# A graph attention layer on one core: nodes laid on the partitions by fours in place of twos

## The reference

```
h      = max(layernorm(x), 0)
Wh     = h @ W
e      = leaky_relu((Wh @ a1)[:, None] + (Wh @ a2)[None, :], 0.2)
scores = where(adj > 0, e, -9e15)
out    = x + elu(softmax(scores, axis=1) @ Wh)
```

## Time and profile before

| what | value |
|---|---|
| median of 3 runs | 654.71 us (654.53 to 655.17) |
| the profiled execution's own time | 654.69 us |
| its span in the profile | 652.8 us |
| PE, DVE, ACT busy | 95%, 94%, 96% |
| POOL busy | 13% |
| DMA queue of GpSimd (loads of `adj`) | 98.6% of 16 engines' span |
| read from HBM | 270.60 MB |

### The profile page before, as it was taken

How to read it: one execution, slowest core, us unless ns; L and a number is a source line. 1 busy time by engine, 2 the same in 40 slices (tenths; PEclk the granted TensorE clock), 3 DMA queues, 4 the chain that set the end, 5 groups by cost and what they waited for, 6 DMA issues and landing times.

```text
span 652.8 us, 23363 instructions
## 1 busy us (share of the span) xinstructions
PE 618.5 (95%) x10422; PEld 607.1 (93%) x10422; DVE 614.8 (94%) x651; ACT 623.9 (96%) x357; POOL 81.6 (13%) x149
## 2 busy tenths in 40 slices
PE   4878999999999999999999999999999999989997
PEld 4748999999999999999899999999999999989997
DVE  5899999999999999889999999999999999999997
ACT  5799999899999999999999999999999999999992
POOL 7200200110110110100010110101010110011000
PEclk9987999999999999999999999999999999999999
DMA  9999999999999999999999999999999999999994
GB/s 173 109 108 109 110 108 108 110 109 109 109 108 108 107 107 108 108 108 108 107 108 108 108 108 107 108 107 108 108 108 107 108 107 108 108 108 107 107 97 132
DMA packets 27678, 71.81 MB, mean 110 GB/s; under 512 B 3200, under 2 KB 11136, under 8 KB 27648
## 3 DMA queue, kind: packets, MB, share of 16 engines
q0 software_dynamic: 18576, 67.12, 98.6%
q1 hardware_dynamic: 8608, 4.19, 2.4%
q10 hardware_dynamic: 464, 0.07, 0.1%
HBM read 270.60 MB, written 2.10 MB: 418 GB/s over the span
## 4 chain that ended last, share of the span: by engine, by line
ACT 53%; DMA 17%; PE 12%; issue 9%; DVE 7%; ACTq 1%; POOL 1%; DVEq 0%
ACT work L520 37%; DMA store<-in_adj 16%; ACT work L528 14%; DVE store L721 4%; PE psum L1083 3%; PE psum L1081 3%; PE psum L1061 2%; PE psum L1050 1%; PE psum L1028 1%; ACT last_steps L533 1%; DVE store L739 1%; DVE work L745 1%; DMA x_sb<-in_x 1%; PE psum L1018 1%; ACT V L512 1%
## 5 line engine op out<-in xcount | busy, mean ns | idle before, releaser
L520 ACT ACTIVATE work<-trow,Wh 128x4096 int8<-128x4096 f32 x128 | 494.6, 3867 | 0.0
L1081 PE MATMUL psum<-V,work 128*128 128x130 f16 x4096 | 479.3, 220 | 1.2 <-DVE work L745 1.2
L1083 PE MATMUL psum<-V,work 128*128 128x130 f16 x4096 | 479.2, 220 | 0.0
L1081 PEld LDWEIGHTS psum<-V,work 128*128 128x128 fp8e4 x4096 | 401.9, 98 | 1.5 <-issue 1.5
L1083 PEld LDWEIGHTS psum<-V,work 128*128 128x128 fp8e4 x4096 | 401.8, 98 | 0.0
L721 DVE TENSOR_SCALAR store<-store 128x4096 uint8<-128x4096 int8 x127 | 290.2, 2286 | 4.4 <-DMA store<-in_adj 4.4
L739 DVE SCALAR_TENSOR_TENSOR store<-work,store 128x1024 int32<-128x1024 int32 x128 | 156.5, 1222 | 12.7 <-ACT work L520 10.0
L528 ACT COPY work<-psum 128x1024 int32<-128x1024 int32 x128 | 147.5, 1155 | 7.6 <-PE psum L1061 7.4
L1061 PE MATMUL psum<-identb,store 128*128 128x128 bf16 x2048 | 135.7, 220 | 16.3 <-DVE store L739 13.4
L1061 PEld LDWEIGHTS psum<-identb,store 128*128 128x128 bf16 x2048 | 119.6, 98 | 20.1 <-DVE store L739 10.7
L443 POOL DMA_DIRECT2D store<-in_adj x127 | 71.2, 561 | 510.9 <-DVE store L721 503.3
(11 more groups left out here) (90 smaller groups left out, 146.6 us busy)
## 6 DMA issues: line engine op xcount, KB each, us to landing
store<-in_adj POOLq DMA_DIRECT2D x127, 512.0 KB, 27.6
x_sb<-in_x SPq DMA_DIRECT2D x4, 512.0 KB, 6.2
out_y<-x_sb SPq DMA_DIRECT2D x1, 1792.0 KB, 8.0
store<-in_adj POOLq DMA_DIRECT2D x2, 256.0 KB, 35.3
out_y<-x_sb SPq DMA_DIRECT2D x1, 128.0 KB, 6.0
out_y<-x_sb SPq DMA_DIRECT2D x4, 32.0 KB, 1.6
store<-in_L_gnn_W ACTq DMA_DIRECT2D x4, 16.0 KB, 5.3
a_sb<-in_L_gnn_a ACTq DMA_DIRECT2D x1, 0.5 KB, 4.2
```

The lines of the kernel that those rows point to most:

```text
L520: nc.scalar.activation(sign[:, k % 2].bitcast(I8), trow[:, h * UW:(h + 1) * UW], ACT.Sign, bias=(Wh[:, B, 0:1] if isinstance(B, int) else ...
L1081: nc.tensor.matmul(sums_of[:, 0], up8[:, j // 2, j % 2], V[:, jb, 0:FP], start=begins and j == 0, stop=False, skip_group_check=True)
L1083: last = nc.tensor.matmul(sums_of[:, 1], down8[:, j // 2, j % 2], V[:, jb, VP:VP + FP], start=False, stop=stops and j == HB - 1, skip_grou ...
```

## The change

Four neighbouring nodes share a partition in place of two: node `g * 512 + p * 4 + b` lies on partition `p` in block `4g + b`. The set of rows in a body stays the same; which of them form a tile changes. The rows of `adj` in one tile were rows `2p + b` of 256, so those of neighbouring partitions lay 2 rows (64 KB) apart; now they are rows `4p + b` of 512, 4 rows (128 KB) apart. Each row's piece is still 16 KB in memory. The loads of `x` and the large stores of the result have pieces of 1 KB (four rows) in place of 512 bytes. The transposes of the codes take every second bfloat16 word, and `spread` writes to every fourth word of `trow`. The products, their operands and their order in the queues stay as they are. The general path's loops run over 16 groups of four in place of 32 pairs, so each engine's code for it has four bodies in place of two.

```diff
-        adj_v = adj.rearrange("(i k p b) j -> k b i p j", p=P, b=2, k=KE // 2)
-        out_i = out.rearrange("(i w p b) f -> i p w b f", p=P, b=2, w=2)
+        adj_v = adj.rearrange("(i p b) j -> b i p j", p=P, b=KE)
+        out_i = out.rearrange("(i p b) f -> i p b f", p=P, b=KE)
...
-                xs = x.rearrange("(g p b) f -> p g b f", p=P, b=2)
-                with nc.allow_non_contiguous_dma(reason="pairs of rows of x, 512 bytes each"):
+                xs = x.rearrange("(g p b) f -> p g b f", p=P, b=KE)
+                with nc.allow_non_contiguous_dma(reason="four rows of x, 1 KB each"):
                     for r in range(NR):
-                        sp.dma_start(x_sb[:, out_of(r), :].rearrange("p (g b) f -> p g b f", b=2),
-                                     xs[:, r * PR:(r + 1) * PR]).then_inc(s_x[r], 16)
+                        sp.dma_start(x_sb[:, out_of(r), :].rearrange("p (g b) f -> p g b f", b=KE),
+                                     xs[:, r * RR // KE:(r + 1) * RR // KE]).then_inc(s_x[r], 16)
-                out_p = out.rearrange("(g p b) f -> p g b f", p=P, b=2)
+                out_p = out.rearrange("(g p b) f -> p g b f", p=P, b=KE)
...
-                    sp.dma_start(out_p[:, i * KE // 2:j * KE // 2],
-                                 x_sb[:, i * KE:j * KE, :].rearrange("p (g b) f -> p g b f", b=2)).then_inc(s_out, 16)
+                    sp.dma_start(out_p[:, i:j],
+                                 x_sb[:, i * KE:j * KE, :].rearrange("p (g b) f -> p g b f", b=KE)).then_inc(s_out, 16)
...
-                    sp.dma_start(out_i[NI - 1, :, b // 2, b % 2], x_sb[:, (NI - 1) * KE + b]).then_inc(s_last, 16)
+                    sp.dma_start(out_i[NI - 1, :, b], x_sb[:, (NI - 1) * KE + b]).then_inc(s_last, 16)
...
-                    pool.dma_start(adj_ring[:, k % RT, :].bitcast(F8W), adj_v[b // 2, b % 2][i, :, h * UW:(h + 1) * UW])\
+                    pool.dma_start(adj_ring[:, k % RT, :].bitcast(F8W), adj_v[b][i, :, h * UW:(h + 1) * UW])\
                         .then_inc(s_adj[k % RT], 16)
...
-                    nc.scalar.activation(trow[:, r * TR * P:(r + 1) * TR * P].rearrange("p (g q b) -> p g b q", q=P, b=2),
-                                         t_ps[r].rearrange("p (g b q) -> p g b q", q=P, b=2), ACT.Copy)\
+                    nc.scalar.activation(trow[:, r * TR * P:(r + 1) * TR * P].rearrange("p (g q b) -> p g b q", q=P, b=KE),
+                                         t_ps[r].rearrange("p (g b q) -> p g b q", q=P, b=KE), ACT.Copy)\
...
                     for g in range(GU):
-                        last = nc.tensor.transpose(into[:, g * P:(g + 1) * P], mine[:, g * P:(g + 1) * P], identb[:, :])
+
+                        c = g // 2 * 2 * P + g % 2
+                        last = nc.tensor.transpose(into[:, g * P:(g + 1) * P], mine[:, c:c + 2 * P - 1:2], identb[:, :])
```

More of the change, by code:

```diff
@@ L44, in build_gat @@
     HB = JB // 2
-    NW = JB // 2
     UW = N // 2
@@ L280, in rows @@
             return what[bass.ds(w, 1), b].rearrange("o p j -> p (o j)")
-        adj_b = adj.rearrange("(w p b) j -> w b p j", p=P, b=2)
-        x_b = x.rearrange("(w p b) f -> w b p f", p=P, b=2)
-        out_b = out.rearrange("(w p b) f -> w b p f", p=P, b=2)
+        adj_b = adj.rearrange("(w p b) j -> w b p j", p=P, b=KE)
+        x_b = x.rearrange("(w p b) f -> w b p f", p=P, b=KE)
+        out_b = out.rearrange("(w p b) f -> w b p f", p=P, b=KE)
         def general_sync(sp):
@@ L289, in general_sync @@
                 sp.sem_inc(g_out, ONE)
-                with sp.Fori(0, NW) as w:
-                    for b in range(2):
-                        sp.wait_ge(g_read, ONE + w * 2 + b)
+                with sp.Fori(0, NI) as w:
+                    for b in range(KE):
+                        sp.wait_ge(g_read, ONE + w * KE + b)
                         sp.dma_start(A, rows(adj_b, w, b)).then_inc(g_adj, 16)
-                        sp.wait_ge(g_res, ONE + w * 2 + b)
+                        sp.wait_ge(g_res, ONE + w * KE + b)
                         sp.dma_start(xt, rows(x_b, w, b)).then_inc(g_x, 16)
@@ L299, in general_scalar @@
                 all_done(act)
-                with act.Fori(0, NW) as w:
-                    for b in range(2):
-                        i = w * 2 + b
+                with act.Fori(0, NI) as w:
+                    for b in range(KE):
+                        i = w * KE + b
                         act.wait_ge(g_dve, i * DSTEPS + 6)
@@ L323, in general_vector @@
                 nc.vector.tensor_copy(Wh1, Wh[:, :, 3:FW]).then_inc(g_Wh1, 1)
-                with dve.Fori(0, NW) as w:
-                    for b in range(2):
-                        i = w * 2 + b
+                with dve.Fori(0, NI) as w:
+                    for b in range(KE):
+                        i = w * KE + b
                         def after(k):
@@ L371, in general_tensor @@
                 pe.wait_ge(g_Wh1, 1)
-                with pe.Fori(0, NW) as w:
-                    for b in range(2):
-                        i = w * 2 + b
+                with pe.Fori(0, NI) as w:
+                    for b in range(KE):
+                        i = w * KE + b
                         pe.wait_ge(g_res, ONE + i)
@@ L384, in general_tensor @@
                                 jb = r * RR + j
-                                c = jb // 2 * 2 * P + jb % 2
+                                c = jb // KE * KE * P + jb % KE
                                 last = nc.tensor.transpose(half[r % 2][:, j * P:(j + 1) * P],
-                                                           score[:, c:c + 2 * P - 1:2], ident[:, :])
+                                                           score[:, c:c + KE * (P - 1) + 1:KE], ident[:, :])
                             last.then_inc(g_round, 1)
@@ L463, in _ @@
                     pool.dma_start(adj_ring[:, RT - 1, n * TW // 2:(n + 1) * TW // 2].bitcast(F8W),
-                                   adj_v[b // 2, b % 2][NI - 1, :, h * UW + n * TW // 2:h * UW + (n + 1) * TW // 2])\
+                                   adj_v[b][NI - 1, :, h * UW + n * TW // 2:h * UW + (n + 1) * TW // 2])\
                         .then_inc(loaded, 16)
```

## The result

The changed kernel takes 656.18 us (median of 12 runs, 654.97 to 656.88) against 654.71 (654.45 to 655.22). The ratio is 1.002 with a 95% interval of 1.0013 to 1.0028: slower by 1.5 us, where 0.3 us less was forecast. The profiled execution took 656.88 us with a span of 654.8.

The account below looks back on a forecast made before the run. The prediction took the stream of `adj` loads to bound the kernel, with engines close behind. Its sum: 654.71 - 0.3 (start) + 0 (loads) + 0 (transposes) + 0 (spreads, 0.6 under cover) = 654.4 us; range 653.4 to 656.4.

Parts of the forecast that it names:

- What bounds the kernel: Whole run: the DMA stream of `adj` sets the end at 4.88 us a tile, engines close behind at 4.62 us a unit.
- Loads of `adj` at 0: 128 tile loads: rows 128 KB apart in place of 64 KB cost 0, as the DMA engines' pace looks constant.
- transposes at 0: TensorE's 2048 code transposes: a 4-byte step costs 0; at most 41 ns each, 84 us in all.
- The rule of the Trainium skill: Loads of `adj`: large power-of-two row distances lose rate; its table costs nothing at 128 KB. Rival of slower loads: 667 us, 6%.
- Load of `x`, 0.3 us: Start of the kernel: 1 KB pieces land `x` and start the `adj` loads 0.3 us earlier; bounds 0 and 1.1 us.
- The spreads: ScalarE's eight table copies: writing every fourth word costs another 78 ns each, 0.6 us in all, hidden by the cover.
- the upper bound: Spreads priced by L581's scattered access, 0.92 ns a word: 0.94 us a spread, 7.5 us in all.
- The cover: Whole run: how much slower the engines could be for nothing, about 1.8 us, from TensorE's idle time between 560 and 630 us.
- the spreads' rival: ScalarE's spreads much slower: tables ready 7.5 us later, 5.7 us come out, 660.1 us; chance 4%.
- Its small case: Slower spreads with only the last four on the path: 3.8 - 1.8 = 2.0 us come out, 656.4 us.
- the stated range: Kernel time from 653.4 to 656.4 us, a little beyond the likeliest case's 653.6 to 655.6.
- The signs of being wrong: Landings over 4.89 us apart: row distance; VectorE not waiting late, TensorE at 99%: engines; L503 near 2 us: spreads.

Follow-up runs that it names:

- the rows alone: Kernel before with only the loads of `adj` changed, taken from rows 128 KB apart: 654.74 us, ratio 1.0002.
- the experiment: Changed kernel with copies of 1024 words at various steps added ahead of the first spread; float32 writes four words apart cost 0.94 us more, kernel time not given.
- all spreads twice: Kernel before with a plain copy of 1024 words ahead of each of its eight spreads and a wait between: 657.99 us, ratio 1.005.
- the spreads alone: Kernel before with only its eight spreads changed, writing to every fourth word of `trow`: 655.54 us, ratio 1.0019.

## Why the prediction was wrong, point by point

- **What bounds the kernel: right.** The loads of `adj` set the end before, and the engines were close behind. Taking the first loads forward gained time, and delays of the engines cost none until they passed 3.85 us.
- **Loads of `adj` at 0, transposes at 0: right**, each shown alone on the chip. The rule of the Trainium skill (DMA: Bandwidth & Descriptors, Latency and other measured facts) on row distances, cited in the prediction, costs nothing at 128 KB here: 654.74 us and 108 GB/s with the rows alone.
- **Load of `x`, 0.3 us: right for the landing**, 4.29 in place of 4.62 over seven traces each. In the time of the kernel it isn't told from noise: with the spreads undone the rest of the change gives 654.59 against 654.66. Its issue also became cheaper, 2.33 us for four in place of 3.86.
- **The spreads: this step failed.** "I take another 78 ns each, 0.6 us in all." They cost 937 ns each (2032 - 1095), 7.5 us in all, which was the upper bound to the tenth. The value was carried on from a step of two words as if the further step cost as much as the first; instead the price comes in beyond 8 bytes and is full at 16. A row for the dear side was there: L581, which takes words 272 bytes apart, 0.92 ns each, and the experiment gives 0.92. I used it as the bound and chose the other. The Trainium skill (SBUF — State Buffer, the note on cachelines) was cited as speaking against it: full rate needs two accesses in a 16-byte line. I gave the rival 4 in 100 all the same. For float32 the runs agree (two words to a line 1.07 us, one 1.96). For float16 they don't: with two elements to a line the copy took 2.43 us against 1.02.
- **The cover: mis-sized too.** "The cover is about 1.8 us over the whole run", from TensorE's idle time between 560 and 630 us. It measured 3.85 us, and the 4.4 us of VectorE's waits, which the prediction had in hand as its own evidence, was the better row. TensorE was the wrong engine to take it from. ScalarE is the one that is busy for all 300 us between 200 and 500, and without waits for tiles TensorE was busy for 69.38 us of those 70 and not for 68.8. This error made the spreads' rival dearer (660.1 us) than it is. Its small case (656.4) was near the result by luck: it has four spreads on the path and a cover of 1.8, where all eight were on it and the cover was twice that. The result lies inside the stated range for the same reason only; the forecast had the wrong sign.
- **The sum as it should have been:** at most 7.5 us of spreads, of which 5.8 reached the units, less 3.85 of cover: +2.0 us, the difference of the two profiled spans. The medians differ by 1.5.
- **The signs of being wrong: right.** "L503 near 2 us the spreads", VectorE no longer waiting for tiles and TensorE at 99% late in the run all showed, and named the cause before any experiment.

The changed kernel's times spread over 1.9 us and the old one's over 0.8. It fits that the end now hangs on the start of the engines, with 600.0 us behind it, and that this start moves from one execution to the next: with the spreads in pairs and the old order of loads the signs behind the last spread started between 46.83 and 48.95 us in four traces, while their spans stayed between 652.4 and 653.0. The cover hid that before. It isn't shown execution by execution, and the five runs with all spreads twice lie within 0.4 us. Part of the movement is on TensorE, in its transposes of the third part of `x`. In the changed kernel's execution and in that of the spreads alone:

```profile
13.05 1.96 PE L1017 MATMUL psum<-ident,work 128*128 128x128 f32 x8
```

```profile
13.02 1.08 PE L1018 MATMUL psum<-ident,work 128*128 128x128 f32 x8 [0.17 <-POOL work L450]
```

The granted clock reads 1.00 (2.4 GHz) there in both. Later it fell to 0.50 (1.2 GHz) at about 34 us, before and after, when TensorE had worked for 0.3 us between 32 and 34, and rose again at some 37.5 us before and 40.5 after. What makes either differ stays open; no run held it apart from the rest.

## What to carry to other kernels

A transfer of layout has a side that shows (pieces of DMA, transposes) and a side that doesn't: the small copies that put tables into the new order. Ask of each write and read how many bytes lie between neighbours, and if a float32 step is over 8 bytes (or a float16 step over 2), price it by the dearest scattered row of the trace, not by going on from the last step; better, keep the writes consecutive and put the step where it is free. Where a stream of loads sets the end, the total wait of the engine that takes the tiles is, within some 0.5 us here, the delay that the others may have for nothing. When the start of the stream is moved, look at what shares the DMA engines with it.

## What the runs showed of the hardware

- 1024 float32 words written to SBUF by ScalarE: 1.02 and 1.07 us at 4 and 8 bytes apart, 1.51 at 12, 1.96 at 16, and level beyond (0.92 ns a word more than plain). VectorE's writes: 1.21, 1.22, 1.50 and 1.95 us. ScalarE's reads of SBUF: 1.06, 1.12 and 2.01 us at 4, 8 and 16 bytes.
- No cost showed for TensorE's weight loads of bfloat16 words 4 bytes apart (98 ns), ScalarE's reads of PSUM four words 512 bytes apart in turn (1022 ns), and TensorE's float32 writes to PSUM 16 bytes apart (273 ns).
- Float16 writes of ScalarE are dear much sooner: 1.02, 1.30, 2.43 and 4.69 us for 1024 elements at 2, 4, 8 and 16 bytes apart.
- A queue with large pieces held up one with small pieces on the same DMA engines. With one tile of `adj` (16 KB pieces) on order beside `x` (1 KB pieces), the third part of `x` was waited for until 13.74 us in place of 8.53, about the 4.9 us of a whole tile. The engines moved 114 to 137 GB/s from 7 to 11 us, near the pace of `adj`, and 322 to 354 from 12 to 14 us.
